# Top-16 attention in a four-layer tower: products with the values in four runs of two heads per tile, in place of two runs of four heads

## What is computed

```python
q, k, v = jnp.split(x @ qkv_w.T + qkv_b, [c, 2 * c], axis=-1)      # then split into 8 heads
logits = jnp.einsum('bmd,bpd->bmp', q * scale, k)
_, idx = lax.top_k(logits, 16)
attn = jax.nn.softmax(jnp.einsum('bmd,bmkd->bmk', q * scale, k[idx]), axis=-1)
out = jnp.einsum('bmk,bmkd->bmd', attn, v[idx])                    # heads joined again
return out @ wo_w.T + wo_b
```

## Time and profile before

| | us |
|---|---|
| median of 3 runs (lowest, highest) | 1506.72 (1487.54, 1507.91) |
| the profiled execution | 1506.79 |
| its span in the trace | 1505.0 |
| DVE busy in the span | 1159.5 |
| PE busy in the span | 1180.9 |

### The profile page before, as it was taken

One profiled execution on the slowest core, in us unless ns is written; L12 is line 12 of the kernel. 1 busy time (PEld: TensorE's weight loads), 2 busy tenths in 40 slices (PEclk: granted clock), 3 DMA queues, 4 the chain that ended last, 5 costly groups with the idle time before them and its releaser, 6 DMA issues. The chain is left out here.

```text
span 1505.0 us, 30283 instructions
## 1 busy us (share of the span) xinstructions
PE 1180.9 (78%) x10544; PEld 810.9 (54%) x10544; DVE 1159.5 (77%) x2164; ACT 745.9 (50%) x1184; POOL 657.4 (44%) x569
## 2 busy tenths in 40 slices
PE   5878999998699878887787788777778786758661
PEld 3735566665489767544444444444444444647551
DVE  5676765554535698799999999999999995768884
ACT  4243434342135411377767677767676765014661
POOL 2133324141375651245555555555555553216144
PEclk9899999999699999999998999999998987869995
DMA  4090000001168400000000000000000000003882
GB/s 133 1 262 2 2 2 3 2 3 51 48 177 227 130 25 0 1 1 1 1 0 0 0 0 0 0 0 0 0 0 0 0 0 0 1 7 113 220 239 74
DMA packets 83643, 65.02 MB, mean 43 GB/s; under 512 B 14202, under 2 KB 74004, under 8 KB 83284
## 3 DMA queue, kind: packets, MB, share of 16 engines
q1 hardware_dynamic: 63124, 46.86, 11.3%
q0 software_dynamic: 4096, 8.40, 2.0%
q10 hardware_dynamic: 16320, 8.40, 1.9%
HBM read 43.70 MB, written 22.28 MB: 44 GB/s over the span
## 5 line engine op out<-in xcount | busy, mean ns | idle before, releaser
L1206 POOL TENSOR_TENSOR ta_ex<-ta_ex,ta_left 128x1024 f32<-128x1024 f32 x128 | 301.5, 2356 | 290.9 <-ACT ta_left L1139 290.9
L1020 PE MATMUL ta_ps_s<-ta_kT,ta_qz 128*128 (+1 forms) x512 | 290.4, 697 | 30.9 <-ACT ta_ex L1123 30.2
L1051 PE MATMUL ta_ps_t<-consts,ta_ex 128*128 128x128 f32 x1024 | 142.5, 283 | 101.2 <-POOL ta_ex L1206 42.6
L1051 PEld LDWEIGHTS ta_ps_t<-consts,ta_ex 128*128 128x128 f32 x1024 | 113.5, 144 | 172.2 <-POOL ta_ex L1206 133.2
L1239 DVE MAX8 ta_top<-ta_ps_s 128x8 f32<-128x1024 f32 x128 | 156.2, 1221 | 31.2 <-PE ta_ps_s L1020 31.0
L1123 ACT ACTIVATE ta_ex<-ta_ps_s,ta_ntop 128x1024 f32<-128x1024 f32 x128 | 142.4, 1112 | 64.8 <-DVE ta_left L1245 53.2
L1020 PEld LDWEIGHTS ta_ps_s<-ta_kT,ta_qz 128*128 128x128 f32 x512 | 98.3, 213 | 123.3 <-issue 118.5
L1245 DVE MATCH_REPLACE8 ta_left<-ta_top,ta_ps_s 128x1024 f32<-128x1024 f32 x128 | 155.4, 1214 | 0.0
L1250 DVE MAX8 ta_top<-ta_left 128x8 f32<-128x1024 f32 x128 | 154.6, 1208 | 0.0
L1255 DVE MATCH_REPLACE8 ta_left<-ta_top,ta_left 128x1024 f32<-128x1024 f32 x128 | 154.6, 1208 | 0.0
L1139 ACT ACTIVATE ta_left<-ta_left,ta_ntop 128x1024 f32<-128x1024 f32 x128 | 146.3, 1143 | 0.9
(11 more groups left out here) (639 smaller groups left out, 2536.1 us busy)
## 6 DMA issues: line engine op xcount, KB each, us to landing
l1f_arena<-in_L_ffn_W_dram SPq DMA_DIRECT2D x46, 256.0 KB
l3e_packed<-l3f_packed SPq DMA_DIRECT2D x64, 160.0 KB, 3.0
l3f_rows<-l1f_zero SPq DMA_DIRECT2D x2, 2048.0 KB, 13.3
l3e_x<-l3f_rows SPq DMA_DIRECT2D x32, 128.0 KB, 3.2
l3e_outs<-l3e_y ACTq DMA_DIRECT2D x32, 128.0 KB, 3.2
l1f_rows<-l1f_zero SPq DMA_DIRECT2D x2, 1472.0 KB, 9.5
l1f_arena<-l1f_rows SPq DMA_DIRECT2D x46, 64.0 KB, 3.7
l1e_outs<-l1e_y ACTq DMA_DIRECT2D x46, 64.0 KB
```

What stands on the lines that cost most here:

```text
L1020: ins = pe.matmul(ps_s[:, i % 2, half * BANK:(half + 1) * BANK], qz[:, odd, h, :], kT[:, grp, bass.ds(at.key0[i // PAIR] + half * BANK, BA ...
L1051: ins = pe.transpose(ps_t[:, j * P:(j + 1) * P], ex[:, i % 4, j * P:(j + 1) * P], m.ident)
L1206: pool.tensor_tensor(ex[:, i % 4, :], ex[:, i % 4, :], left[:, i % 4, :], ALU.subtract).then_inc(kept, 1)
```

## The change

The value products of a tile now come in four runs of two heads. A table VALUES, indexed by h, says which heads are multiplied in step h: heads 0 and 1 in step 2, heads 2 and 3 in step 4, heads 4 and 5 in step 6, heads 6 and 7 in step 7. A run has 8 blocks of keys times 2 heads, 16 matmuls (32 records); 64 matmuls a tile as before, with the same operands, and each head writes the same place as before. In steps 2, 4 and 6 the run needs only items whose copies the transposes of the same step have already waited for, so it has no wait of its own; in step 7 it waits as before. The wait for acc_out moves from step 3 to step 2. ACT, DVE and POOL have the same instructions in the same order.

```diff
+    VALUES = [(), (), (0, 1), (), (2, 3), (), (4, 5), (6, 7)]
...
-                    if h % 4 == 3:
+                    if h == 2:
+                        pe.wait_ge(acc_out, at.tile0 + (i // TH + 1))
+                    if h == TH - 1:
                         pe.wait_ge(exT_in, n + 1)
-                        if h == 3:
-                            pe.wait_ge(acc_out, at.tile0 + (i // TH + 1))
-                        grp = h // 4
-                        for j in range(CH):
-                            for q in range(4):
-                                ins = pe.matmul(ps_o[32 * q:32 * q + 2 * TW, grp * P:(grp + 1) * P], vseq[:, j, 4 * grp + q, :],
-                                                exT[(i - 3 + q) % 8][:, j, :], start=(j == 0), stop=(j == CH - 1))
+                    for j in range(CH):
+                        for head in VALUES[h]:
+                            q, grp = head % 4, head // 4
+                            ins = pe.matmul(ps_o[32 * q:32 * q + 2 * TW, grp * P:(grp + 1) * P], vseq[:, j, head, :],
+                                            exT[(i - h + head) % 8][:, j, :], start=(j == 0), stop=(j == CH - 1))
```

## The result

| | before | after |
|---|---|---|
| median of 3 runs, us | 1506.72 (1487.54 to 1507.91) | 1527.74 (1525.30 to 1531.16) |
| span of the profiled execution, us | 1505.0 | 1526.0 |

The ratio is 1.0197, 95% interval 1.0106 to 1.0288 (the quotient of the medians is 1.014); the width comes from the one run of 1487.54 among the three of before. A second comparison on another chip gave 1.0224 (1.0038 to 1.041). The forecast was 1527. On one of the chips used further down, the runs of the kernel before fell into a faster group (4 of 13, median 1560.6) and a slower one, and the ratios, and the medians of before beside them, go by the faster.

What follows compares the result with a forecast made beforehand. DVE was taken as the bound, busy 74.8 of 78.5 us a loop body, its waits coming from slow-clock logits. Loop +15, first tile +3, last tile +2: +20 us on 1506.8, so 1527 us; 0.8 range 1493 to 1541.

Steps and rivals of the forecast that it cites:

- Length of a run: Value products on PE: a run of two heads takes 1.75 us like one of four, adding 3.5 us a tile.
- The transpose of o: On PE behind step 4's new run: 1.4 us later, delaying ACT and later logits, using up DVE's 1.4 us slack exactly.
- The 0.4 us that I had for accT: DVE's wait for accT at the reciprocal, 0.4 us a body at full clock.
- 1.2 us a body at full clock: DVE's waits in a loop body from the new order: 0.7 and 0.1 us for logits, 0.4 for accT; none before.
- The number of slow stretches: Half-clock PE stretches in a loop body fall from 4 to 2.7, each now reaching DVE whole at 1.6 us.
- The sum of the two: Full-clock waits plus slow stretches: 5.5 us a body against 3.7, +1.8; +2.2 taken, +15 us over 7 bodies.
- First tile: PE, which also has projections there, needs 4.7 us an item against DVE's 4.65: +3 us (0 to 5).
- Last tile: At half clock, step 6's run takes 3.5 us and holds up the transposes of step 7: +2 us.
- Rival 1: In the loop: no slow stretch is left, only 1.2 us of full-clock waits a body: -12, 1495 us; chance 0.12.
- Rival 2: Value products: two groups go as fast as four, a run takes 0.9 us, slack stays: about 1494 us; chance 0.07.
- rival 3: In the loop: slow stretches stay as many, half-filled products don't hold the clock: +32, 1539 us; chance 0.15.
- rival 4: Nothing arrives: PE has 16 us idle a body and ACT's waits take up the shift: 1507 us; chance 0.08.

Runs made afterwards that it cites:

- e1: Kernel before, value runs kept in steps 3 and 7 but each going through two heads first, then the other two: 1529.5 us, ratio 1.0126 to the kernel before.
- e2: Changed kernel with runs of four heads again, heads 0 to 3 in step 4, 4 to 7 in step 7: 1520.1 us, ratio 1.0054 to the kernel before.
- e4: Kernel before plus one unused 256-column matmul ahead of the transposes of each step but 0 and 4: 1483.0 us, ratio 0.9809 to the kernel before.
- e6: Changed kernel plus one unused 256-column matmul ahead of the transposes of steps 1, 2, 4 and 6: 1576.1 us, ratio 1.0012 to the kernel before.
- e3: Changed kernel with the run of heads 2 and 3 moved behind the transpose of o in step 5: 1491.5 us, ratio 0.9859 to the kernel before.
- e10: Kernel before with clock-holding fillers, plus four unused matmuls ahead of the transpose of o in step 5: 1572.5 us, ratio 1.0128 to the kernel before.

## Why the prediction came out right, point by point

- *Length of a run.* Right: 1.94 us for 32 records, where 1.75 and a tail was the estimate, 14 records in half a microsecond where four heads had 29, and e1 shows that the order of the same matmuls makes it so. PE's busy time rose by 34 us, not by some 50: clean bodies of the two lengths (this kernel 63.9 us, e2 56.8) do differ by 7.1 us, which is 57 us over 16 tiles, but 15 slow stretches fewer, at about 1.6 us each, give 24 back.
- *The transpose of o.* Right in kind, short in size. The predicted delay was 1.4 us, "the slack is used up exactly, DVE does not wait yet". Against DVE, the logits that began 3.4 us ahead of it before (871.48, and 874.84) now begin 1.4 ahead (964.68, and 966.77 - 0.65 = 966.12): 1.9 us later in place of 1.4. The step that was short is the way from the transposes of step 4 to the transpose of o: I had 4.5 us (859.87 to 864.4), it takes 5.0 (951.19 to 956.16). The transposes do start earlier, but the logits behind them follow 1.19 us later and not 0.93, as ACT's exponential, which frees their buffer, ends only at 952.18 (951.07 + 1.11); they take 1.90 from start to start, not 1.72, and the run 1.88, not 1.75. With the slack gone this reaches DVE: 0.65 us of wait in every tile that I had at about nothing. For the logits behind the fetch it is 1.68 where I had 0.7: ACT's fetch starts 1.96 us behind DVE's max (973.39, 971.43), and 0.36 behind it in the clean body of e4 (1029.71, 1029.35); with the 0.65 that DVE is late itself, this is 2.2 us later than at full clock before, where I had 1.2. The 0.4 us that I had for accT did not come. So the term "1.2 us a body at full clock" measured 3.0 (3.2 with fillers). This is the step that was mis-sized.
- *The number of slow stretches.* 2.7 a body in the prediction, 11 and 9 in seven bodies measured, 1.3 to 1.6. The proportion of open gaps (6 to 4 of 8) is not how it goes; a settled body often has none. Their price, 1.6 us each with the slack gone, measured 1.5 to 1.7.
- *The sum of the two.* Predicted +2.2 a body (the terms gave 1.8, and I chose 2.2), measured 19.0 / 7 = +2.7. The two errors have opposite signs: 3.2 - 1.2 = 2.0 us too little for the order, and for the stretches 19 / 7 = 2.7 us against 4.3, 1.6 too much. The forecast of 1527 is so close partly by luck.
- *First tile.* +3 predicted; the max of item 9 starts 2.1 us later (676.91 against 674.81). But that of item 8 starts at the same time (669.94, 669.91), and e2, with runs of four, has the same gap between the two (6.9 us, against 4.9 before): the size is right and the reason, PE overloaded in the first tile, is not. *Last tile.* +2 predicted, about -2 measured: the transposes of step 7 are indeed held by a run at half clock (3.63 us, from 1283.34), but the last run then goes at full clock, and the loop's end has fewer slow stretches.
- *Rival 1, the clock stays up*, half happened, and its price was wrong because it rested on the same 1.2 us: e6 has that clock and is no faster than the kernel before, where the rival said 12 us. Rival 2 is refuted by the runs' length, rival 3 by the count of slow stretches, rival 4 by ACT's 3.17 us and by the total.

That ACT's copy of oT passes the delay on was argued from the order; e3 (delay away, long runs kept) and e10 (delay alone) show it at the full clock. What stays open is why slow stretches come in some bodies of the changed kernel and not in others that have the same order.

## What to carry to other kernels

Splitting a packed group of small matmuls costs PE time although their number stays: count rounds per column group, not matmuls. When work is put into an idle gap of an engine, look at what stands directly behind it and who waits for that in order; here the place of one run against one 0.3 us transpose decided between 2% slower and 1.4% faster. And when a stage's waits come with a falling clock, price the order and the clock apart, once with fillers that hold the clock, before judging a reordering by its total.

## What the runs showed of the hardware

Fillers of one 256-column matmul in the gaps with transposes only, 12 in 75 us, took away all slow stretches of the loop: 0 in place of 26. PE's busy time fell at the same time, 1178.1 us in place of 1180.9, as the loop's logits no longer took 3.5 us in place of 1.9; with more work the engine was less busy.

The pace of the value products depends on how many column groups take turns. Records of two groups come at (0.5 + 0.273) / 14 = 55 ns, those of four at 27 ns: a round of one matmul in each group takes 0.11 us either way. In the run of e1 the rounds of the second pair of heads start before those of the first are over (22 records in the half microsecond in the middle), so its 64 records take 3.22 us from start to start and not 2 x 1.88.
